# Flamingo block on one core: the rows of a batch are asked for two batches ahead of their spreads instead of one

## What is computed

```python
# part 1: gated "cross attention": a 3-tap convolution over positions, each tap scaled by a cosine
f   = layernorm(x)                                     # over the 1024 positions
sim = stack([cos(ctx, ctx shifted right), cos(ctx, ctx), cos(ctx, ctx shifted left)])  # over the 128 channels
inp = stack([f padded by 1, shifted by k for k in 0..2])            # 128 channels x 3 taps = 384 rows
x   = x + tanh(g_xattn) * einsum('bit,oi->bot', inp * repeat(sim, 128), weight)
# part 2: gated mixture of 8 low-rank experts, top 2 of 8 by a softmax router
h   = layernorm(x) @ A.T                               # 8 experts x rank 16 = 128 values a token
x   = x + tanh(g_ffn) * 0.5 * (h * gate of its expert) @ Bm
```

## Time and profile before

| | before |
|---|---|
| median of 3 runs | 285.1 us (283.19, 285.10, 285.16) |
| the profiled execution's own time | 283.32 us |
| its span (first to last instruction) | 281.4 us |
| granted TensorE clock, mean share of full speed | 0.933 |
| TensorE matmul busy | 228.2 us (81%) |
| VectorE busy | 161.5 us (57%) |
| ScalarE busy | 111.9 us (40%) |
| GpSimd busy | 80.2 us (29%) |

### The profile page before, as it was taken

The page is one execution under the profiler, slowest core; times in us unless marked ns, Lnnn a source line. Parts: engine busy times, 40 slices in busy tenths (PEclk is TensorE's granted clock), DMA queues, the critical chain, the costliest instruction groups (busy, mean ns, idle before and its releaser), DMA issues.

```text
span 281.4 us, 3557 instructions
## 1 busy us (share of the span) xinstructions
PE 228.2 (81%) x1050; PEld 130.0 (46%) x1050; DVE 161.5 (57%) x403; ACT 111.9 (40%) x192; POOL 80.2 (29%) x219
## 2 busy tenths in 40 slices
PE   7879499696996985879679788788959599998972
PEld 5733246364543543545354334445426355554651
DVE  1479666862752644747366173694717265858453
ACT  3799381736270350433516245044604306302120
POOL 1555610317043040212603414031312204212141
PEclk9999899999599896899959999979998979999999
DMA  7797041602132160121212012120401220101113
GB/s 235 267 353 313 0 176 49 223 3 82 75 139 95 76 229 9 72 82 75 81 57 85 19 77 81 76 79 5 149 8 77 83 80 4 79 6 75 75 75 149
DMA packets 9565, 27.94 MB, mean 99 GB/s; under 512 B 1965, under 2 KB 2600, under 8 KB 9548
## 3 DMA queue, kind: packets, MB, share of 16 engines
q1 hardware_dynamic: 9548, 27.73, 26.9%
HBM read 18.67 MB, written 8.39 MB: 96 GB/s over the span
## 4 chain that ended last, share of the span: by engine, by line
PE 32%; DVE 22%; SPq 18%; issue 18%; DMA 7%; ACT 2%; POOL 1%; DVEq 0%; POOLq 0%
PE bank L916 14%; SPq L312 14%; DVE pt L715 8%; PE bank L941 6%; DMA rows<-rows 4%; DVE x L722 3%; PE bank L897 3%; PE bank L934 3%; DVE x L759 2%; DMA et<-ctx 2%; PE bank L857 2%; DVE pr L633 2%; SPq L302 1%; DVE bn L727 1%; PE bank L950 1%
## 5 line engine op out<-in xcount | busy, mean ns | idle before, releaser
L715 DVE TENSOR_TENSOR pt<-xn,bank 128x512 f32<-128x512 f32 x96 | 63.0, 679 | 87.1 <-issue 60.9
L916 PE MATMUL bank<-pt,wT 128*128 128x512 f32 x192 | 107.8, 654 | 0.0
L941 PEld LDWEIGHTS bank<-aT,xT 128*128 128x128 f32 x256 | 39.4, 216 | 19.6 <-issue 15.3
L916 PEld LDWEIGHTS bank<-pt,wT 128*128 128x128 f32 x192 | 35.4, 211 | 22.2 <-issue 16.8
L550 ACT ACTIVATE hs<-bank 128x128 f32<-128x128 f32 x16 | 4.4, 277 | 95.6 <-PE bank L941 95.6
L941 PE MATMUL bank<-aT,xT 128*128 128x136 f32 x256 | 40.8, 309 | 1.6 <-ACT xT L543 1.3
L418 POOL CAST topf<-topi 128x2 f32<-128x2 uint32 x16 | 3.0, 184 | 113.1 <-DVE topi L746 113.1
L543 ACT ACTIVATE xT<-bank 128x512 f32<-128x512 f32 x32 | 19.1, 596 | 40.2 <-PE bank L934 39.7
L897 PE MATMUL bank<-rows,sel 9*128 9x512 bf16 x72 | 10.1, 411 | 25.0 <-DMA rows<-rows 25.0
L934 PEld LDWEIGHTS bank<-ident,x 128*128 128x128 f32 x128 | 16.0, 146 | 22.7 <-issue 12.9
L759 DVE TENSOR_TENSOR x<-bank,x 128x512 f32<-128x512 f32 x32 | 21.7, 679 | 4.7 <-PE bank L961 4.7
(11 more groups left out here) (91 smaller groups left out, 252.7 us busy)
## 6 DMA issues: line engine op xcount, KB each, us to landing
et<-ctx SPq DMA_DIRECT2D x16, 512.0 KB, 5.7
xt<-x SPq DMA_DIRECT2D x16, 512.0 KB, 3.3
out<-x SPq DMA_DIRECT2D x15, 512.0 KB, 2.6
rows<-rows SPq DMA_DIRECT2D x108, 6.0 KB
aT_in<-expert_aT SPq DMA_DIRECT2D x1, 544.0 KB, 9.9
bm_in<-expert_b SPq DMA_DIRECT2D x1, 512.0 KB, 11.8
out<-x SPq DMA_DIRECT2D x2, 256.0 KB, 2.0
sel<-select SPq DMA_DIRECT2D x1, 216.0 KB, 10.0
```

Of the source, the lines that this page charges most:

```text
L715: nc.vector.tensor_tensor(pt[:, i, :], xn[:, n % 2, h * HALF + t:(h + 1) * HALF + t], sim_bank(k)[:, :], ALU.mult).then_inc(mod_done, 1)
L916: nc.tensor.matmul(conv_ps[h][:, :], wT[:, t * P:(t + 1) * P], pt[:, i, :], start=(t == 0), stop=(t == TAPS - 1)).then_inc(tap_done, 1)
L941: last = nc.tensor.matmul(h_ps[:, 0:ER + E], xT[:, n % 2, c, :], aT[:, c, :], start=(c == 0), stop=(c == KC - 1))
```

## The change

In iteration n the queue now asks for the rows of batch n+2 instead of batch n+1. The first copies (batch 4) so stand in iteration 2, the last (batch 15) in iteration 13. The number of DMAs, their sources, targets and waits, and every other engine's list stay as they are. Every tap runs in full float32 before and after.

```diff
@@ -352,8 +352,8 @@
                     load_x(n + 3)
                 for e in {1: (8, 9), 2: (10, 11), 4: (12, 13), 5: (14, 15)}.get(n, ()):
                     load_e(e)
-                if ABREAST <= n + 1 < B:
-                    load_rows3(n + 1)
+                if ABREAST <= n + 2 < B:
+                    load_rows3(n + 2)
             for n in range(B - 4, B - 1):
                 store(n)
             for h in range(2):
```

## The result

| | before | changed |
|---|---|---|
| median | 284.5 us (4 runs, 283.19 to 285.16) | 251.58 us (4 runs, 251.21 to 252.06) |
| profiled execution, its own time | 283.32 us | 251.59 us |
| its span | 281.4 us | 249.3 us |
| granted TensorE clock, mean | 0.933 | 0.979 |

The changed kernel takes 0.885 of the time (95% interval 0.881 to 0.889): 32.9 us less. The forecast was 250.5 us, with 246 to 258 as its range.

A forecast was written before the change was run, and what follows sets the result against it. Waits bound the kernel, chiefly TensorE's for row copies queued too late. Iterations 3 to 12 fall from 171.5 to 138.0 us, 33.5 less: 283.3 to 249.8, taken as 250.5, range 246 to 258.

The forecast's parts named there:

- The wait removed: TensorE's spreads waiting for the row copies, 25.0 us in ten waits, would go or shrink to one short wait.
- The sum by iteration: Iterations 3 to 12, each priced without the wait and mostly at full clock: 138.0 us against 171.5, 33.5 less.
- The product: VectorE's context product in iterations 3, 4, 7 and 8 would make the hidden-value transpose wait over 1 us; price 1.14.
- The clock: TensorE would run at full clock, 1.00, from iteration 3 on, as iteration 6 did before.
- rival B: Short gaps keep TensorE's clock low, 1.57 us per affected iteration: 263 us if all eight, 256 to 258 if half; chance 0.13.
- The bound by the clock: At most 16.0 us back from some 33.6 us at the lower clock in seven iterations.
- What stands behind the copies: SyncE's queue stops some 5 us in iterations 6 and 10; later load and store cost nothing, bound 2 us each.
- One wait that was costed at nothing: The moved copies' new wait for all spreads of batch n, taken as covered by the wait for the second residual.
- the span: The whole profiled span, forecast to fall from 281.4 by 33.5 to 247.9 us.
- Rival D: The wait for batch n's spreads comes so late that the copies land as before: 284 to 285 us, chance 0.03.
- Rival E: SyncE's queue becomes the bound if copies issue more slowly: slower kernel, 300 us at 2.0 each; chance 0.02.
- two thresholds: Issue time of the nine copies: the queue decides from 11.1 us, kernel slower than before from about 16.4.

The follow-up runs named there:

- order_only: The kernel before, rows still asked one batch ahead, but their nine copies queued ahead of the loads of x and context: 251.41 us, ratio 0.886.
- after_again: The changed kernel run once more with no edit, as partner for the other runs: 251.57 us, ratio 0.885 to the kernel before.
- product_late: The changed kernel with VectorE's context product of step 3 put behind the finish and the residual: 250.5 us, ratio 0.879 to the kernel before.
- extra9: The changed kernel with nine further copies of the same size, read by nobody, queued behind each batch's nine: 256.1 us, ratio 0.897.
- product_pool: The changed kernel with context products 8, 10, 12 and 14 on GpSimd instead of VectorE: 246.18 us, ratio 0.866 to the kernel before.
- before_filled_half: The kernel before, copies as late as there, with 22 useless matmuls where TensorE waited for them: 276.8 us, ratio 0.972.

## Why the prediction was right

*The wait removed*: right, all ten are gone. *The sum by iteration*, 138.0 us forecast and 138.29 measured:

| iterations | forecast | changed |
|---|---|---|
| 3, 7 | 13.07 | 13.46, 13.07 |
| 4, 8 | 15.62 | 15.55, 15.53 |
| 5, 9 | 13.96 | 13.90, 13.90 |
| 6, 10 | 14.44 | 14.36, 14.66 |
| 11, 12 | 11.93 | 11.92, 11.94 |

Iteration 3 is the one that is clearly off, by 0.39. The forecast gave it the length of 7, but it has three matmul rows more (60 against 57): one more set of output products (L959 to L961) falls into it. So iterations 7 to 10 don't quite repeat 3 to 6. The method that gave the sum was to find an iteration that had already been free of the defect (13) or free of its side effect (6, 8 and 9 at full clock), and to subtract only the wait. *The product* that is late next: right in place and size. Iterations 3 and 4 wait 1.36 and 1.34 us for it; the timeline of TensorE shows it in 7 and 8, the wait of 1.34 now in both, where iteration 8 alone had it:

```profile
129.47 0.30 PE L950 MATMUL bank<-ident,hw 128*128 128x128 f32 x1 [1.34 <-DVE x L759]
...
143.81 0.30 PE L950 MATMUL bank<-ident,hw 128*128 128x128 f32 x1 [1.34 <-DVE x L759]
```

*The clock*: rival B didn't come; full clock in nine of ten, and iteration 10, which has the short gaps of the earlier trace rows, fell again. It cost 0.30 us, not the 1.57 that B put on each. The choice of full clock for these iterations went by one example, iteration 6, and was in part luck: with the copies in time it was iteration 10 that fell in order_only and after_again too, iteration 6 in product_late, both in extra9 and neither in product_pool. In the profile of the changed kernel TensorE was busy for 1.94 us of the 3.12 before 106.12, less than in the earlier trace rows, and the clock stayed at 1.00. What decides it isn't shown. The rule of the Trainium skill cited in the prediction ("TensorE: Matmul & The Clock Gate", "A second HAM failure mode: psum-queue depth-cycling") agrees with this trace at one place of four. *The bound by the clock* of 16.0 us comes near the busy time: TensorE's fell by 13.1, and iteration 10 kept 1.5. As a price on the path it was too high: before_filled_half puts that at 7.2.

*What stands behind the copies*: right for the group iterations. The queue of the changed kernel, iterations 2 and 3, and 6 and 7:

```profile
56.61 6.22 SPq L312 DMA_DIRECT2D rows<-rows  x9
63.93 0.33 SPq L302 DMA_DIRECT2D xt<-x  x1
...
106.83 0.33 SPq L302 DMA_DIRECT2D xt<-x  x1
112.05 6.16 SPq L312 DMA_DIRECT2D rows<-rows  x9
118.25 0.42 SPq L317 DMA_DIRECT2D out<-x  x1
121.19 0.33 SPq L302 DMA_DIRECT2D xt<-x  x1
```

The first copies are over before the load of iteration 3. In iteration 6 the queue stops from 107.16 to 112.05, 4.9 us against "some 5" forecast, is free for the store at 118.25, and the load of x of iteration 7 follows at 121.19 without being late; no wait of ScalarE for x is in the list of waits. One wait that was costed at nothing exists: in iteration 13, where no load of x stands in front, the queue waits 2.6 us for the spreads of the batch that used the buffer. It is covered too: nobody waits for those copies.

*What was off*: the span, 249.3 for 247.9. The ten iterations explain 0.3. Most of the rest lies ahead of iteration 3. Up to the second residual of batch 2, the kernel before and then the changed one:

```profile
0.00:62.20 62.20, 51.22 (x283) 29.27 (x283) 40.22 (x113) 37.00 (x53) 23.73 (x50) 0.97 0.51 183
```

```profile
0.00:63.21 63.21, 52.86 (x283) 30.39 (x283) 40.01 (x112) 36.99 (x53) 23.17 (x50) 0.95 0.50 181
```

The same matmul rows, 1.64 us more of TensorE busy at a clock of 0.95 against 0.97, and 1.01 us more time. It isn't the change: iteration 2, in which the first copies are now issued, takes 12.06 us against 12.07, so the difference is there before any instruction was moved, and the second profile of the changed kernel reaches this point at 61.98, at 0.94. The start varies from one execution to the next by a microsecond or more; why isn't shown, and the mean clock alone doesn't give it. *Rival D* is excluded by the waits. *Rival E* was rightly thought far off, its mechanism is real, and the two runs lie on the sides that it gave: 13.4 us of queue work in an iteration slow the plain ones, 20 us make the kernel slower than before. The point between wasn't located. (Its two thresholds for the nine issues, 11.1 and 16.4 us, count 0.8 for the rest of a turn; with the 7.1 that it states they are 11.0 and 16.2, which changes nothing.) It had the copies themselves in mind as what would come late; it is the store behind them.

## What to carry to other kernels

A queue that issues in order makes a transfer as late as the last wait in front of it. Small transfers that an engine needs soon belong ahead of one that has to wait itself and that nobody needs for an iteration; putting them there (order_only) or asking a batch earlier gave the same 33 us, and neither added an instruction. To price the removal of a repeated wait, look for one repetition in which it didn't occur, take that whole repetition as the new length, and then look in the others for what it would uncover: here a product that had cost 1.1 us in one iteration and then cost as much in four.

## What was not expected of the hardware

- Time at the lower clock cost about half of its bound on the path: some 33.6 us at 1.2 GHz were bounded at 16.0 us and gave back 7.2, after 0.85 lost in an iteration that fell anew and with VectorE's waits uncovered; iteration 10 lost nothing at 0.89 (15.22 and 15.21 us).
- The same instructions with the same gaps don't get the same clock each time: with the copies in time, iteration 6 or 10, both or neither ran in part at 1.2 GHz.
- A product of 1023 columns takes 1.22 us on VectorE and 1.89 on GpSimd, and moving four of them to the engine that takes longer made the kernel 5 us faster; VectorE's multiplication beside it stayed at 680 ns.
- 74 us of further small copies inside SBUF, beside loads and stores of 512 KB, left the issue time of nine copies at 6.1 to 6.6 us. They moved only 54 KB more a batch, so this says nothing of heavy traffic; what was felt is the time that the queue spends on issuing.
